# A fused attention and experts kernel: its first two block programs written out by hand, with several one-time steps placed elsewhere

## What is computed

```python
x = x + cross_attention_16_heads_and_MLP(layernorm(x), ctx)     # L0_xattn: softmax over 64 keys, then relu(out @ W1 + b1) @ W2 + b2
x = x + experts(layernorm(x))                                   # L0_ffn
x = x + cross_attention_1_head(layernorm(x), ctx)               # L1_xattn
x = x + (layernorm(x) @ weight.T + pooled(layernorm(x)) @ disha)  # L1_ffn

# experts: 8 experts share wi and wo, each adds a rank-16 term; a gate picks 2
logits = h @ gate_w.T + gate_b
for e in range(8):
    inter = h @ wi.T + bi + (h @ lora_A[e].T) @ lora_B[e].T
    out += gate_e * (relu(inter) @ wo.T + bo)
```

## Time and profile before

| | us |
|---|---|
| median of three runs | 328.65 |
| the three runs | 328.63, 328.65, 330.46 |
| profiled execution | 328.38 |
| its span, first to last instruction | 326.2 |
| TensorE busy in the span | 312.0 (96%) |
| VectorE busy | 231.3 (71%) |
| ScalarE busy | 173.2 (53%) |
| GpSimd busy | 145.4 (45%) |

### The profile page before, as it was taken

One profiled execution on the slowest core, in us unless ns is written; L12 is line 12 of the kernel. 1 busy time (PEld: TensorE's weight loads), 2 busy tenths in 40 slices (PEclk: granted clock), 3 DMA queues, 4 the chain that ended last, 5 costly groups with the idle time before them and its releaser, 6 DMA issues.

```text
span 326.2 us, 6486 instructions
## 1 busy us (share of the span) xinstructions
PE 312.0 (96%) x2497; PEld 284.3 (87%) x2497; DVE 231.3 (71%) x644; ACT 173.2 (53%) x355; POOL 145.4 (45%) x150
## 2 busy tenths in 40 slices
PE   7989998999999999999999999999999999999982
PEld 5749896999979998899989997999899988999771
DVE  4865675846877877867796687678777769456766
ACT  4367645682676348455656367635753564434511
POOL 1655763544072805472264507280628134713441
PEclk9999999999999999999999999999999999999997
DMA  7589820004000320013000400042002200000000
GB/s 249 174 248 349 185 66 2 0 18 107 8 1 2 81 82 0 2 43 95 29 0 21 109 34 0 2 97 67 2 0 55 76 3 1 2 15 19 0 34 32
DMA packets 14702, 18.85 MB, mean 58 GB/s; under 512 B 2224, under 2 KB 11312, under 8 KB 14416
## 3 DMA queue, kind: packets, MB, share of 16 engines
q1 hardware_dynamic: 12640, 14.99, 16.8%
q10 hardware_dynamic: 2032, 3.44, 3.0%
HBM read 9.51 MB, written 2.62 MB: 37 GB/s over the span
## 4 chain that ended last, share of the span: by engine, by line
PE 84%; DVE 5%; ACT 4%; DMA 2%; SPq 2%; POOL 1%; issue 1%; DVEq 0%; POOLq 0%; ACTq 0%
PE psI L302 13%; PE psI L458 13%; PE psP L311 12%; PE psI L311 11%; PE psS L311 7%; PE psT L302 4%; PE psP L393 3%; PE psT L326 3%; PE psS L379 2%; PE psP L394 2%; PE psT L525 2%; PE psS L356 2%; PE psI L620 1%; PE psP L612 1%; DMA xin<-in_x 1%; PE psP L434 1%
## 5 line engine op out<-in xcount | busy, mean ns | idle before, releaser
L1429 POOL TENSOR_TENSOR rs<-ve,mhalf 128x2 f32<-128x2 f32 x30 | 21.9, 730 | 93.8 <-DVE ve L1054 93.8
L1448 POOL TENSOR_TENSOR hid_l<-r,hid_h 128x512 fp32r<-128x512 f32 x32 | 40.8, 1289 | 15.4 <-ACT hid_h L850 15.4
L1133 DVE SCALAR_TENSOR_TENSOR r<-psI,nbi,r 128x256 f32<-128x256 f32 x60 | 25.8, 479 | 25.1 <-PE psI L458 25.1
L458 PE MATMUL psI<-at_h,lb_h 128*128 128x256 f32 x120 | 36.4, 304 | 2.0 <-DVE at_l L1125 1.5
L1442 POOL TENSOR_TENSOR hs_l<-hs,hs_h 128x512 fp32r<-128x512 f32 x16 | 20.8, 1302 | 35.5 <-ACT hs_h L830 35.4
L458 PE MATMUL psI<-at_l,lb_h 128*128 128x256 f32 x120 | 33.8, 282 | 0.0
L458 PE MATMUL psI<-at_h,lb_l 128*128 128x256 f32 x120 | 33.8, 282 | 0.0
L1074 DVE RECIPROCAL rec<-psP 128x256 f32<-128x256 f32 x16 | 28.1, 1753 | 4.8 <-PE psP L394 4.8
L845 ACT ACTIVATE r<-psI,first 128x256 f32<-128x256 f32 x60 | 24.1, 468 | 13.7 <-PE psI L458 13.5
L458 PEld LDWEIGHTS psI<-at_h,lb_h 128*128 128x128 f32 x120 | 22.6, 188 | 8.6 <-issue 5.0
L814 ACT ACTIVATE ex<-psS 128x512 f32<-128x512 f32 x32 | 18.9, 595 | 18.3 <-PE psS L379 18.2
(11 more groups left out here) (258 smaller groups left out, 866.5 us busy)
## 6 DMA issues: line engine op xcount, KB each, us to landing
stack<-qu_h SPq DMA_DIRECT2D x60, 64.0 KB, 2.0
xin<-in_x SPq DMA_DIRECT2D x8, 256.0 KB, 2.8
stack<-qu_l SPq DMA_DIRECT2D x30, 64.0 KB, 2.0
out<-x ACTq DMA_DIRECT2D x7, 256.0 KB, 2.0
raw_wi<-in_wi SPq DMA_DIRECT2D x1, 1024.0 KB, 9.0
raw_wo<-in_wo SPq DMA_DIRECT2D x1, 1024.0 KB, 12.2
kv<-in_kv SPq DMA_DIRECT2D x2, 384.0 KB, 7.9
raw_w<-in_w ACTq DMA_DIRECT2D x1, 512.0 KB, 8.4
```

What stands on the lines that cost most here:

```text
L458: last = mm(bank[:, k * T:(k + 1) * T], (WH, WL)[x]["lb"][:, 0, f * P:(f + 1) * P], AT[y][:, which, :], start=False, stop=q == 2, skip_gro ...
L1133: last = V.scalar_tensor_tensor(out=R1[:, f, :], in0=bank[:, k * T:(k + 1) * T], scalar=nbi[:, f:f + 1], in1=R1[:, f, :], op0=MAX, op1=ADD)
L1429: G_.tensor_tensor(rs[:, :], ve[:, :], mhalf[:, :], ALU.pow).then_inc(S(f"ln{j}_rs"), 1)
L1448: G_.tensor_tensor(HL[:, two, :], R1[:, two, :], as32(HH[:, two, :]), ALU.subtract).then_inc(S("hidl"), 1)
```

## The change

Bodies 0 and 1 become `first_body` and `second_body`, written out on all four engines; the loop runs `body` for blocks 2 to 7, with the same steps in the same order as before.

In the first body the first attention's four score steps stand ahead of both `a_attend`; part of block 1's queries goes ahead of the hidden layer; `f_gate(0)` follows the second norm, four fillers and two score steps of block 1; the other two score steps and `a_attend(1, 0)` stand behind `f_base(0, 0)`; `f_lora_transposes(0)` ends up ahead of `f_base(0, 1)`. Body 0 has 14 fillers, and 5 stand ahead of it.

`values1`, `folded_keys` and `fold_turn` move to the second body, `fold_means` and `fold_values` to later places in it, and so do the steps on the other engines that follow them; `high_weights("wo")` and the low part of wo move there too. Temporary tiles (`kt1`, `passing`, `kv1`) get other addresses, some results another PSUM bank. Two of the four transfers that stack block 1's low queries are issued from ScalarE's queue in place of SyncE's.

Core of the diff (banks, addresses and the unrolled loop's old branches left out):

```diff
--- before
+++ after
@@ sync @@
-                stack_q(b, 1)
+                stack_q(b, 1, (0, 1) if b == 1 else range(GPC))
...
@@ tensor @@
-            def a_queries(b):
+            def a_queries(b, high=True, low=True):
...
-            def a_hidden(b, u):
+            def a_hidden(b, u, banks=S_, high=True, low=True):
...
-                    last = values(I_(1)[:, b * D:(b + 1) * D], kv1[:, WV1:WV1 + 2 * D], b)
+                    last = values(T_(1)[:, b * D:(b + 1) * D], kv1[:, WV1:WV1 + 2 * D], b)
...
             def folded_keys():
                 pe.wait_ge(S("kt1"), 1)
-                pe.wait_ge(S("crow"), 1)
...
-                    last = mm(I_(0)[:, 0:P], cols[:, BQ1 + k:BQ1 + k + 1].broadcast_to([P, P]),
+                    last = mm(T_(0)[:, KC * P:(KC + 1) * P], cols[:, BQ1 + k:BQ1 + k + 1].broadcast_to([P, P]),
...
+            def first_body():
+                a_scores(0, 0)
+                a_scores(0, 1)
+                for d in (2, 3):
+                    filler(I_(0), 2)
+                    a_scores(0, d)
+                filler(I_(0), 2)
+                a_attend(0, 0)
+                a_attend(0, 1)
+                pe.wait_ge(S("v0"), BATCH)
+                filler(T_(0), 2)
+                transposes(1, 1, T_(1))
+                filler(T_(0), 2)
+                a_queries(1, low=False)
+                a_hidden(0, 0, I_, low=False)
+                a_queries(1, high=False)
+                a_hidden(0, 0, I_, high=False)
+                a_hidden(0, 1, I_)
+                a_out(0, 0)
+                pe.wait_ge(S("ex"), DPAIRS)
+                a_row_scores(1, 0)
+                a_row_scores(1, 1, T_)
+                a_out(0, 1)
+                a_max_transposes(1, S_(0))
+                constant_row()
+                keys1()
+                transposes(2, 0, T_(1))
+                filler(I_(1), 4)
+                a_scores(1, 0)
+                a_scores(1, 1)
+                f_gate(0, 1)
+                pe.wait_ge(S("kt1"), 1)
+                f_base(0, 0)
+                a_scores(1, 2)
+                a_scores(1, 3)
+                pe.wait_ge(S("crow"), 1)
+                a_attend(1, 0, T_(0))
+                f_lora_transposes(0)
+                f_base(0, 1)
+
+            def second_body():
+                f_first(0, 0)
+                f_first(0, 1)
+                pe.wait_ge(S("x1"), 1)
+                a_attend(1, 1)
+                f_second(0, 0)
+                f_second(0, 1)
+                values1()
+                pe.wait_ge(S("o32"), KC + 1)
+                folded_keys()
+                a_hidden(1, 0)
+                pe.wait_ge(S("v1"), 1)
+                transposes(1, 2, T_(1))
+                f_base(0, 2)
+                a_hidden(1, 1)
+                f_first(0, 2)
+                f_base(0, 3)
+                a_queries(2)
+                f_second(0, 2)
+                f_first(0, 3)
+                a_out(1, 0)
+                a_row_scores(2, 0)
+                a_out(1, 1)
+                f_second(0, 3)
+                pe.wait_ge(S("g_in"), BATCH + 1)
+                fold_turn()
+                fold_means()
+                f_out(0, 0)
+                a_row_scores(2, 1)
+                f_out(0, 1, low=False)
+                fold_values()
+                pe.wait_ge(S("gw"), 1)
+                transposes(2, 1, T_(1))
+                f_out(0, 1, high=False)
+                a_max_transposes(2)
+                f_gate(1, 2)
+                pe.wait_ge(S("vv_l"), 2)
+                c_turn(0)
+                f_base(1, 0)
+                f_base(1, 1)
...
-            filler(I_(0), 3)
-            for i in range(NBLK):
-                body(i, i - 1 if i >= 1 else None, i - 2 if i >= 2 else None, i + 1 if i + 1 < NBLK else None)
+            filler(I_(0), 5)
+            first_body()
+            second_body()
+            for i in range(2, NBLK):
+                body(i, i - 1, i - 2, i + 1 if i + 1 < NBLK else None)
...
@@ scalar @@
+            def folded_in():
+                act.wait_ge(S("gb_ps"), 1)
+                for b in range(BATCH):
+                    A(GWR[:, :, b * (KEYS + D):b * (KEYS + D) + KEYS],
+                      T_(0)[:, 0:KC * P].rearrange("p (c b k) -> p c b k", c=KC, b=BATCH)[:, :, b, :],
+                      ACT.Identity).then_inc(S("g_in"), 1)
+                A(gb[:, :], T_(0)[:, KC * P:(KC + 1) * P], ACT.Identity).then_inc(S("g_in"), 1)
...
+            def first_body():
+                for d in range(DPAIRS):
+                    exps(0, d)
+                normalise(1, 1, XIN)
+                high(1, 1, XTA, T_(1))
+                attended(0, 0)
+                high_weights("w2")
+                attended(0, 1)
+                high_weights("wi")
+                hidden(0, 0, I_)
+                hidden_high(0, 0)
+                queries(1)
+                hidden(0, 1, I_)
+                hidden_high(0, 1)
+                high_weights("ga")
+                high_weights("lb")
+                act.wait_ge(S("ql"), 2 * KC)
+                for g in (2, 3):
+                    stack_q(1, 1, g)
+                maxima(1, S_(0))
+                normalise(2, 0, XMID)
+                high(2, 0, XTF, T_(1))
+                exps(1, 0)
+                exps(1, 1)
+                sorted_exps(0)
+                exps(1, 2)
+                exps(1, 3)
+
+            def second_body():
+                lora_high(0)
+                high_weights("wo")
+                first_relu(0, 0)
+                first_relu(0, 1)
+                normalise(1, 2, XIN)
+                attended(1, 0)
+                sum_high(0, 0)
+                attended(1, 1)
+                sum_high(0, 1)
+                act.wait_ge(S("v1"), 1)
+                A(VV[0][:, 0:2 * BATCH:2, :], r3(v1, BATCH), ACT.Identity).then_inc(S("vv_h"), 1)
+                folded_in()
+                hidden(1, 0)
+                hidden_high(1, 0)
+                high(1, 2, XTA, T_(1))
+                first_relu(0, 2)
+                hidden(1, 1)
+                queries(2)
+                hidden_high(1, 1)
+                first_relu(0, 3)
+                act.wait_ge(S("v1t_ps"), 1)
+                A(v1t[:, :], T_(0), ACT.Identity).then_inc(S("v1t"), 1)
+                sum_high(0, 2)
+                sum_high(0, 3)
+                act.wait_ge(S("gw"), 1)
+                A(gw_h[:, :], gw[:, :], ACT.Identity).then_inc(S("gw_h"), 1)
+                normalise(2, 1, XMID)
+                act.wait_ge(S("vw_ps"), 1)
+                A(VV[0][:, 1:2 * BATCH:2, :], T_(0).rearrange("p (b n) -> p b n", b=BATCH), ACT.Identity).then_inc(
+                    S("vv_h"), 1)
+                high(2, 1, XTF, T_(1))
+                maxima(2)
+                high(3, 0, XTC, T_(0))
+                sorted_exps(1)
...
@@ vector @@
+            def first_body():
+                dve.wait_ge(S("x_in"), 2 * 16)
+                norm_stats(1, 1, XIN)
+                attended(0, 0)
+                attended(0, 1)
+                low(1, 1, XTA, T_(1))
+                low_weights("wi", 1, 2)
+                queries_low(1)
+                row_max(1, 0)
+                row_max(1, 1, psT)
+                first_residual(0)
+                dve.wait_ge(S("x1"), 1)
+                norm_stats(2, 0, XMID)
+                low_weights("ga")
+                low_weights("lb")
+                constant()
+                low(2, 0, XTF, T_(1))
+                experts(0)
+                gates(0)
+
+            def second_body():
+                lora_low(0)
+                dve.wait_ge(S("x_in"), 3 * 16)
+                norm_stats(1, 2, XIN)
+                attended(1, 0, T_(0))
+                hidden_sum(0, 0)
+                attended(1, 1)
+                hidden_sum(0, 1)
+                values_bias()
+                dve.wait_ge(S("vv_h"), 1)
+                V.tensor_tensor(VV[1][:, 0:2 * BATCH:2, :], r3(v1, BATCH), as32(VV[0][:, 0:2 * BATCH:2, :]),
+                                SUB).then_inc(S("vv_l"), 1)
+                low(1, 2, XTA, T_(1))
+                dve.wait_ge(S("ld_wc"), 16)
+                V.tensor_tensor(GWR[:, :, KEYS:KEYS + D], GWR[:, :, KEYS:KEYS + D],
+                                late[:, D:2 * D].unsqueeze(1).broadcast_to([P, KC, D]), ADD).then_inc(S("wc_sum"), 1)
+                hidden_sum(0, 2)
+                queries_low(2)
+                row_max(2, 0)
+                hidden_sum(0, 3)
+                first_residual(1)
+                dve.wait_ge(S("x1"), 2)
+                norm_stats(2, 1, XMID)
+                dve.wait_ge(S("gw_mean"), 1)
+                V.tensor_tensor(GWR, GWR, T_(1)[:, 0:GW].unsqueeze(1).broadcast_to([P, KC, GW]), SUB).then_inc(
+                    S("gw"), 1)
+                row_max(2, 1)
+                low(2, 1, XTF, T_(1))
+                dve.wait_ge(S("vv_h"), 2)
+                V.tensor_tensor(VV[1][:, 1:2 * BATCH:2, :], T_(0).rearrange("p (b n) -> p b n", b=BATCH),
```

(95 more changed lines are left out.)

441 lines of the change are left out of this document (123 added, 318 removed).

## The result

The changed kernel takes 331.73 us (median of 4, 331.06 to 332.55) where the one before takes 328.79 beside it: ratio 1.0066, 95% interval 1.0034 to 1.0098. That is 2.9 us slower, inside 1%. The forecast was 329.9, 1.25 us slower, with a range to 331.8: the sign and the class are right, the size is less than half of what came. Of the executions further down, one of e6_no_fill (335.30 us) and one of e7_values_back (337.34), both over 1.5% longer than the fastest of their kernel, are left out of the medians.

A forecast was written before the change was run, and what follows sets the result against it. TensorE, busy in nearly all of the time, was taken as the bound: -0.45 us in the first body, new waits of 0.55, 0.4 and 0.75, net +1.25, giving 329.9 us, range 327.4 to 331.8.

The forecast's parts named there:

- rival 3: Body 1: VectorE becomes the bound, its margins of 0.3 to 0.7 us used up; 331.0 to 332 us, chance 0.16.
- rival 1: The forecast itself: early gain lost to new waits in body 1; 329.9 us, range 329.0 to 330.8, chance 0.50.
- a gain of 0.45 ahead of body 1: First body, at equal work: TensorE 0.45 us earlier, as the first LoRA product no longer waits.
- Start to hidden layer: Body 0, first scores to hidden layer: begins at 28.5, not 28.26 us, with TensorE idle about 0.7.
- To constant_row: Body 0, hidden layer to constant_row: 8.15 us instead of 9.0, so constant_row begins at 36.65, 0.6 earlier.
- Second norm: First body, ahead of the gate: norm ready in time without values1, no wait, transposes 0.45 us.
- Experts' wait: First body, gate logits to masked input: VectorE's 2.83 us covered by TensorE's 3.0; first LoRA product at 50.0, no wait.
- Fillers: Body 0: fillers go from 10 to 14, 1.72 us more on TensorE, paid where no wait is covered.
- (a): End of body 1: ScalarE's v1t copy, waiting for fold_turn, delays sum_high 2 and 3; 0.4 us, low halves 0.15 more.
- (b): End of body 1: c_turn waits for X2, behind vv_h, xtf_l and vv_l; 0.4 us, between 0 and 0.8.
- (c): Start of body 2: c_scores(0) waits for xtc_l, behind gw_l, moved after experts(1); 0.75 us, between 0.3 and 2.0.
- GpSimd beside VectorE: At gw_l: a GpSimd collision either slows or stops VectorE; taken as 0, worst case 1.28 us more.

The follow-up runs named there:

- e6_no_fill: Changed kernel without the four fillers ahead of block 1's first scores (a_scores(1, 0)): 330.29 us.
- e7_values_back: Changed kernel with values1 and its bias back in the first body, values1 where the four fillers stand: 331.70 us.
- e1_again: The changed kernel once more, no edit, beside the kernel before: 331.89 us, ratio 1.0076.
- e2_keys_late: Changed kernel with the three transfers reading batch 1's keys issued behind block 1's stack, not ahead of it: 331.35 us.
- e8_end_fixed: Changed kernel with three queue reorderings in the second body, one for each new wait at its end: 329.61 us, ratio to the kernel before 1.0018.
- e11_early_attend: Changed kernel with end waits reordered, key reads behind stack, second attended half first, no four fillers, old block 0 attention order, later wi split: 328.67 us.
- e13_values_early: Changed kernel with end waits reordered, key reads behind stack, second attended half first, values1 replacing four fillers, old block 0 attention order, later wi split: 328.42 us.

## Why the prediction was right in sign and small in size

The range holds the result by 0.07 us, and e1_again's 331.89 lies outside it: that it holds is luck. The time is in the band of rival 3, whose mechanism didn't come; the mechanism is that of rival 1, new waits in body 1, but outside the 329.0 to 330.8 given to it, because a gain of 0.45 ahead of body 1 was counted on and a loss came.

Held against the profiles, step by step. Forecasts are on the clock of the kernel before; e2_keys_late's profile stands for an execution with the start at 18.8 and no wait for the stack.

- *Start to hidden layer.* Forecast: 9.7 us after the first scores, with 0.7 idle. Measured 9.84 with 0.69. Right; so was the reading that the fillers ahead of the attention only push VectorE's two reciprocals back.
- *To constant_row.* Forecast 8.15 us, measured 8.39 (29.34 to 37.73). I had taken the hidden layer's waits as unchanged; a new one of 0.26 for hs_h came in front of a_out.
- *Second norm.* Costed at no wait "with time to spare". From the start of transposes(2, 0) to the fillers it took 0.77 us and not 0.45. xn was ready at 42.51 only:

```profile
41.42 1.09 ACT L827 ACTIVATE xn<-xmid,nmr,rs 128x256 f32<-128x256 f32 x2 [1.44 <-POOL nmr L1513]
```

  Without values1 in front, keys1 alone no longer covers the norm: about 0.3. I had named this cover and taken no wait all the same, without pricing the norm's chain.
- *The transfers.* The step that failed outright. I counted what TensorE does before a_scores(1, 0) and never asked when its stack lands, though this step, at 49.81 before, is now reached at 44.7. It waits 0.62 us in one profile, 2.06 in another, and there the clock goes down too; e8_end_fixed, with the same transfers, doesn't wait.
- *Experts' wait.* Forecast: covered, transposes of the masked input right behind the attention, first LoRA product 6.3 us after the gate's start. Measured 6.55 (45.89 to 52.44), no wait. Right, and it is the gain that the change is for. But the gate itself starts at 45.89 and not at 43.7 (start 0.7, small terms 0.7, stack 0.6, the rest not traced). In e2_keys_late the product starts at 50.89, 0.9 later than forecast, also with no wait.
- *Fillers.* Forecast 1.72 us for four. In e2_keys_late they fill 1.54 (42.14 to 43.68), and without them the time is 1.6 less against e1_again and 1.1 against e2_keys_late (e6_no_fill). Right that they are paid, by 0.2 too dear.
- *(a), (b), (c).* Forecast 0.4 with 0.15, 0.4 and 0.75; measured 0.52 with 0.1, 0.58 and 0.57: 1.7 forecast, 1.77 measured, and e8_end_fixed takes all three away by order alone. Right in place, cause and sum. The rest of body 1 is 0.4 us longer than forecast; I put it down to switches between kinds of products, which I had taken from the old order, but no run shows it.
- *GpSimd beside VectorE.* For (c) I took 0 and had named the worse case from the row of wi_l. gw_l took 0.95 us, the same as alone: no collision there. Elsewhere there was:

```profile
31.03 2.43 DVE L1431 TENSOR_TENSOR wi_l<-raw_wi,wi_h 128x1024 fp32r<-128x1024 f32 x1 [1.69 <-ACT wi_h L918]
...
64.14 2.07 DVE L1362 TENSOR_TENSOR gw<-gw,late 128x512 f32<-128x512 f32 x1
```

  GpSimd's instructions beside them:

```profile
29.96 2.41 POOL L1613 TENSOR_TENSOR w_l<-raw_w,w_h 128x1024 fp32r<-128x1024 f32 x1
33.09 1.51 POOL L1522 TENSOR_TENSOR hs_l<-hs,hs_h 128x512 fp32r<-128x512 f32 x1 [0.71 <-ACT hs_h L865]
...
63.26 2.40 POOL L1613 TENSOR_TENSOR wo_l<-raw_wo,wo_h 128x1024 fp32r<-128x1024 f32 x1
```

  GpSimd's w2_l ran from 29.96 to 32.37, and wi_l ended at 33.46, 1.09 later. In the kernel before it was 1.08 later, though the two had run side by side for 0.65 us there and for 1.34 here; lb_l, of the same width, ended 1.09 behind GpSimd's wo_l there and took 1.22 alone here. The same rest each time behind the end of GpSimd's instruction speaks for the full stop, not for the slower pace. The second row's operation took 0.69 us before the change; GpSimd's wo_l ran until 65.66 beside it, and it ended 0.55 later. It goes the other way round as well: hs_l on GpSimd, 1.29 us otherwise, began at 33.09 while wi_l still ran, took 1.51 and ended 1.14 behind it. So whichever of the two starts later stands still until the other is done, but for some 0.15 us. The Trainium skill (SBUF — State Buffer, "Who interferes with whom") says the same of a VectorE operation with two SBUF inputs and a GpSimd instruction that reads SBUF: the first to issue gets the shared ports for its whole instruction and the other blocks. The traces agree. None of these was on TensorE's path.

The sum then: 1.25 forecast, less 0.2 at (c), + 0.9 in body 0 (0.15 start to hidden, 0.25, 0.3, and 0.2 not traced), + 0.2 for (a) and (b), + 0.4 not traced in body 1 = 2.55. e2_keys_late, which has these and no stack wait in its profile, measured 2.5 above the kernel before (331.35 to 328.83). The stack brings the rest, 0.4 to 0.5 by the medians, and more in single executions. Rival 3 (VectorE the bound of body 1) was not what cost the time here, as no wait stood at a_hidden(1, 0), but its margin was 0.05 us and not the 0.3 of the forecast, and e7_values_back ran straight into it.

## What to carry to other kernels

When a step is moved forward, ask for each of its inputs when it lands, the transfers first: the profile of before shows them only as late as they were then needed, and transfers that nothing waits for yet (here key reads needed from block 4 on) can stand in its way. A one-time step may be cover for its neighbour and slack for another engine: take it away, and both have to be priced. At the end of a body, three one-time operations each placed ahead of an instruction on the path cost 1.7 us, and moving them in the queues gave all of it back.

## What was not expected of the hardware

The small transfers of the stack (64 KB each) took 2.6 to 4.5 us from issue to landing ahead of three reads of 128 KB and 4.1 to 6.6 behind them (3.4 in the kernel before), by and large the more the fuller the DMA engines were; the reads themselves took 9.6 to 12.0 us in the changed kernel and 2.8 to 3.6 once moved (e2_keys_late). And a wait of 1 to 2 us on TensorE can be followed by a loss of as much again: behind 2.06 us of waiting the granted clock was at 0.50 for 3.4 us (e1_again), behind 0.97 and 0.29 us for 6.8 us (e11_early_attend, an execution 2.8 us longer than its median), while 1.50 us before the change and 0.97 in e13_values_early left it at 1.00. What decides between them stays open.
